# An attention and feed-forward kernel: from slot 8 on, the value products stand ahead of the scores

## The reference

```
sim = einsum('bhnid,bhnjd->bhnij', q * scale, kw)   # kw: token 0 and the 5 blocks around
attn = softmax(where(mask, -max, sim))
attn = einsum('gh,bhnij->bgnij', w_th, attn)        # the heads are mixed
out = einsum('bhnij,bhnjd->bhnid', attn, vw)
return out @ w_out + b_out
```

## Time and profile before

| | us |
|---|---|
| time, median of 3 runs | 244.66 (244.61 to 244.81) |
| profiled execution, its time | 244.73 |
| its span, from the first to the last instruction | 242.9 |
| PE busy | 225.3 |
| DVE busy | 177.2 |
| ACT busy | 162.9 |
| POOL busy | 93.2 |
| mean granted clock of TensorE, as a share of the full one | 0.988 |

### The profile page before, as it was taken

The page is one execution under the profiler, slowest core; times in us unless marked ns, Lnnn a source line. Parts: engine busy times, 40 slices in busy tenths (PEclk is TensorE's granted clock), DMA queues, the critical chain, the costliest instruction groups (busy, mean ns, idle before and its releaser), DMA issues.

```text
span 242.9 us, 10011 instructions
## 1 busy us (share of the span) xinstructions
PE 225.3 (93%) x4343; PEld 201.6 (83%) x4343; DVE 177.2 (73%) x461; ACT 162.9 (67%) x311; POOL 93.2 (38%) x111
## 2 busy tenths in 40 slices
PE   7899979999999999999999999998999988989970
PEld 6799869888999999888988888887988877889850
DVE  0774889987777882688667785678567899785874
ACT  2685557776656558975597559884697453888772
POOL 7035205532333351544425254534435264101452
PEclk9999999999999999999999999999999999999995
DMA  6937560020020001100200101010200101000003
GB/s 214 276 97 207 172 150 7 13 57 0 3 58 12 24 3 39 35 26 3 65 3 4 47 25 46 3 46 4 65 6 0 49 3 43 4 0 26 3 3 86
DMA packets 19107, 11.69 MB, mean 48 GB/s; under 512 B 2232, under 2 KB 18168, under 8 KB 18936
## 3 DMA queue, kind: packets, MB, share of 16 engines
q1 hardware_dynamic: 18324, 10.47, 15.3%
q10 hardware_dynamic: 740, 0.59, 0.8%
HBM read 8.91 MB, written 2.10 MB: 45 GB/s over the span
## 4 chain that ended last, share of the span: by engine, by line
PE 56%; DVE 18%; ACT 16%; issue 4%; DMA 2%; POOL 2%; POOLq 0%; SPq 0%; DVEq 0%; ACTq 0%
PE bank L1106 9%; PE bank L1108 8%; PE bank L1107 8%; PE bank L1255 7%; PE bank L1229 6%; DVE CTl L874 5%; PE bank L1213 3%; ACT CTh L577 3%; DVE AT L879 2%; ACT Yb L577 2%; DMA xq<-in_L_attn_x 2%; ACT L668 2%; DVE mx L886 2%; ACT gT L668 2%; PE bank L1299 2%
## 5 line engine op out<-in xcount | busy, mean ns | idle before, releaser
L874 DVE TENSOR_TENSOR CTl<-bank,CTh 128x512 fp32r<-128x512 f32 x64 | 41.0, 682 | 25.3 <-ACT CTh L577 25.1
L577 ACT ACTIVATE Yb<-bank 128x512 f32<-128x512 f32 x64 | 38.4, 600 | 28.3 <-PE bank L1108 27.7
L519 POOL TENSOR_TENSOR E<-E,rc 128x400 f32<-128x400 f32 x32 | 28.4, 889 | 75.5 <-DVE rc L896 75.3
L1106 PE MATMUL bank<-xTh,Gh 128*128 128x256 f32 x128 | 39.7, 310 | 1.7 <-ACT Yb L577 1.4
L720 ACT ACTIVATE E<-E 128x400 f32<-128x400 f32 x32 | 17.3, 539 | 32.1 <-DVE E L888 32.1
L1106 PE MATMUL bank<-CTh,Mh 128*128 128x256 f32 x128 | 37.0, 289 | 1.0 <-DVE CTl L874 1.0
L577 ACT ACTIVATE CTh<-bank 128x512 fp32r<-128x512 f32 x64 | 34.7, 600 | 2.4 <-PE bank L1255 2.4
L1108 PE MATMUL bank<-CTh,Ml 128*128 128x256 f32 x128 | 36.1, 282 | 0.0
L1107 PE MATMUL bank<-CTl,Mh 128*128 128x256 f32 x128 | 36.0, 281 | 0.0
L1107 PE MATMUL bank<-xTl,Gh 128*128 128x256 f32 x128 | 35.8, 279 | 0.0
L1108 PE MATMUL bank<-xTh,Gl 128*128 128x256 f32 x128 | 35.7, 279 | 0.0
(11 more groups left out here) (142 smaller groups left out, 465.0 us busy)
## 6 DMA issues: line engine op xcount, KB each, us to landing
raw<-in_L_attn_x SPq DMA_DIRECT2D x37, 64.0 KB
pt_rows<-PT SPq DMA_DIRECT2D x2, 512.0 KB, 5.3
R<-pt_rows SPq DMA_DIRECT2D x1, 1024.0 KB, 5.0
xr<-in_L_attn_x SPq DMA_DIRECT2D x6, 128.0 KB
out<-y SPq DMA_DIRECT2D x6, 128.0 KB, 1.9
raw<-in_L_attn_x SPq DMA_DIRECT2D x13, 56.0 KB
w_sb<-in_L_attn_w_qkv SPq DMA_DIRECT2D x2, 256.0 KB, 4.8
w_sb<-in_L_attn_w_qkv ACTq DMA_DIRECT2D x2, 256.0 KB, 4.6
```

What stands on the lines that cost most here:

```text
L519: tt(e, e, rc[s % 2][:, :].unsqueeze(2).broadcast_to([P, TILES, WIN]), ALU.mult).then_inc(s_norm, 1)
L577: copy = lambda o, i, **k: nc.scalar.activation(o, i, ACT.Copy, **k)
L874: v.tensor_tensor(ct_view(CTl[s // 4 % 2], s % 4, q), c_view(s, q), ct_view(f32(CTh[s // 4 % 2][:, :, :]), s % 4, q), ALU.subtract).then_i ...
L1106: mm(o, wh, rh, start=start, stop=False, **k)
```

## The change

`TURN = 7` is new. Up to slot 6 nothing changes; slot 7 does the old and the new beginning of work once each. From slot 8 on the order inside a slot is:

- TensorE: `c_part(s - 2)`, `scores(s)` with chunk n's square sum between the score products and the mask when k = 5, `transposes(s - 1)`, feed-forward pieces, `queries(s, 0)`, `o_part`, `down`, `queries(s, 1)`, `x1_T`.
- ScalarE: `ct_hi(s - 2)`, `at_hi(s - 1)`, `y_out(s, 0)`, `squares` when k = 4, Exp, `gelu` when k = 2, `y_out(s, 1)`, the rest.
- VectorE: `ct_lo(s - 2)`, `shift(s)`, `hidden_sum` when k = 5 (it now waits for `down_back` too, which writes the same bank), `at_lo(s - 1)`, `input_scale` and `up_input`, `second_sum` for n = 3, `total(s)`, the rest.

Transposes thus come one slot after their scores, no longer two. Behind the loop only `c_part(30)`, `transposes(31)` and `c_part(31)` are left, and `c_part(31)` takes the two spare banks that slot 30's took. What waits for what else is as it was, the wait for `s_O` in `ct_hi` among it.

```diff
+TURN = 7
         def c_bank(s, q):
-            return bank[(0, 2)[q] if s == 30 else C_BANK[q]]
+            return bank[(0, 2)[q] if s == 31 else C_BANK[q]]
 ...   ScalarE's loop
-                if s > LAG:
+                if LAG < s <= TURN:
                     ct_hi(s - LAG - 1)
-                if 0 < s < O_LAG:
+                if 0 < s < TURN:
                     y_out(s, 0)
-                if s >= LAG:
+                if LAG <= s <= TURN:
                     at_hi(s - LAG)
-                if s == 0 or s >= O_LAG:
+                if s == 0 or s == TURN:
                     y_out(s, 0)
-                if s < O_LAG:
+                if s >= TURN:
+                    ct_hi(s - 2)
+                    at_hi(s - 1)
+                if s > TURN:
+                    y_out(s, 0)
+                if s < TURN:
                     y_out(s, 1)
+                for n, k in ffn(s):
+                    if k == 4 and n < 4:
+                        squares(n, 0)
+                        squares(n, 1)
                 e = E[s % 2][:, :, 0:WIN]
                 act.wait_ge(s_sub, s + 1)
                 nc.scalar.activation(e, e, ACT.Exp).then_inc(s_exp, 1)
-                if s >= O_LAG:
+                for n, k in ffn(s):
+                    if k == 2 and n < 4:
+                        gelu(n, 0)
+                        gelu(n, 1)
+                if s >= TURN:
                     y_out(s, 1)
 ...
-            at_hi(30)
-            ct_hi(29)
+            ct_hi(30)
+            at_hi(31)
             gelu(4, 0)
-            at_hi(31)
-            ct_hi(30)
+            ct_hi(31)
             gelu(4, 1)
-            ct_hi(31)
 ...   VectorE's loop
-                if s > LAG:
+                if LAG < s <= TURN:
                     ct_lo(s - LAG - 1)
-                if s >= LAG:
+                if LAG <= s <= TURN:
                     at_lo(s - LAG)
+                if s > TURN:
+                    ct_lo(s - 2)
+                shift(s)
+                if s == TURN:
+                    ct_lo(s - 2)
                 for n, k in ffn(s):
-                    if k == 5 and n == 3:
+                    if k == 5:
+                        dve.wait_ge(f_back, n + 1)
                         hidden_sum(n)
+                if s >= TURN:
+                    at_lo(s - 1)
                 for n, k in ffn(s):
                     if k == 1:
                         input_scale(n)
                         up_input(n)
-                shift(s)
 ...   TensorE
-            def scores(s):
+            def scores(s, sums=()):
 ...
+                for n in sums:
+                    pe.wait_ge(f_dS, n + 1)
+                    square_sum(n)
 ...
-                need(pe, s_CTl, 60 if s == 31 else 2 * s if s < 30 else 0)
-                if s == 30:
+                need(pe, s_CTl, 2 * s if s < 31 else 0)
+                if s == 31:
 ...   TensorE's loop
-                if 0 < s < O_LAG:
+                if 0 < s < TURN:
                     queries(s, 0)
-                if s >= LAG:
+                if LAG <= s <= TURN:
                     transposes(s - LAG)
-                scores(s)
+                if s > TURN:
+                    c_part(s - 2)
+                scores(s, [n for n, k in ffn(s) if k == 5])
+                if s > TURN:
+                    transposes(s - 1)
 ...
-                if s == 0 or s >= O_LAG:
+                if s == 0 or s >= TURN:
                     queries(s, 0)
-                for n, k in ffn(s):
-                    if k == 5:
-                        square_sum(n)
-                if s == O_LAG:
+                if s == TURN:
+                    c_part(s - 2)
+                    transposes(s - 1)
 ...
                 for n, k in ffn(s):
                     if k == 4 and n < 4:
                         down(n)
+                queries(s, 1)
+                for n, k in ffn(s):
                     if k == 1:
                         x1_T(n)
-                queries(s, 1)
 ...
-                if s >= LAG:
+                if LAG <= s < TURN:
                     c_part(s - LAG)
 
-            transposes(30)
-            o_part(6, 1)
             c_part(30)
             transposes(31)
+            o_part(6, 1)
             o_part(6, 2)
             c_part(31)
```

More of the change, by code:

```diff
@@ L730, in _ @@
                         down_out(n)
-                        squares(n, 0)
-                        squares(n, 1)
                     if k == 1:
@@ L737, in _ @@
                         hidden_high(n, 1)
-                    if k == 2 and n < 4:
-                        gelu(n, 0)
-                        gelu(n, 1)
                     if k == 8 and n < 3:
                         result(n)
-            at_hi(30)
-            ct_hi(29)
+            ct_hi(30)
+            at_hi(31)
             gelu(4, 0)
-            at_hi(31)
-            ct_hi(30)
+            ct_hi(31)
             gelu(4, 1)
-            ct_hi(31)
             x1_hi(5)
@@ L1016, in _ @@
                         up_input(n)
-                shift(s)
                 for n, k in ffn(s):
-                    if k == 5 and n < 3:
-                        hidden_sum(n)
                     if k == 5 and n == 3:
@@ L1059, in _ @@
                         second_norm(n)
-            at_lo(30)
-            ct_lo(29)
+            ct_lo(30)
             at_lo(31)
-            ct_lo(30)
             ct_lo(31)
```

## The result

| | us | ratio to before |
|---|---|---|
| before, median of 4 runs | 244.63 (244.11 to 244.81) | |
| changed, median of 4 runs | 263.08 (259.35 to 265.33) | 1.066 (1.058 to 1.074) |
| changed, profiled execution | 262.44, span 260.6 | |

The change makes the kernel slower, by 6.6% in the ratio and by 18.4 us between the medians; 253.8 was forecast, in a range from 247.5 to 258.5. The direction was right and the size was not.

A forecast was written before the change was run, and what follows sets the result against it. TensorE, busy 93% of the span, was taken to set the pace, with evacuations close behind. Slots 8 to 27 +6.5, slot 7 +0.5 and the end +2.1 sum to +9.1, giving 253.8 us, range 247.5 to 258.5.

The forecast's parts named there:

- plain slot: A loop slot without feed-forward work on TensorE: 5.26 us instead of 5.41, 0.15 less, bounds 0 and 0.3.
- square sums: Slots 16, 20, 24 and 28, between scores and mask: 0.55 us instead of 0.84, 0.29 less each.
- turning in slot 7: Slot 7: the value products move ahead of the output part and wait for at_lo(5), charged +0.5 us.
- slots 8 to 27: Main loop: shorter slots -3.0, square sums -0.9, old waits -6.9, new waits +2.3, five waits +15.0; together +6.5 us.
- end up to T(31): Slots 28 up to transposes(31): the transposes wait for normalising of the slot just before; +0.9 us.
- from T(31) on: After transposes(31): output part (6,1), 1.42 us, now stands there, and the last value products lose 0.2 of waiting; +1.2.
- the five waits: Slots 10, 14, 18, 22 and 26: ct_hi waits for s_O; 8.26 us against 5.26, 3.0 lost each, 15.0 together.
- waits that go and new ones: Slots 8 to 27: old waiting and fringe removed, 6.9 us less; late softmax, up_input and ct_hi add 2.3.
- Clock: Rival, 4%: 2.2 us stands halve TensorE's clock, second query part and value products take twice as long; 8.5 more, 262.3.
- Recovery: Rival, 18%: each wait for s_O costs only 2.26 us, the next slot's slack absorbs VectorE's lateness; 248.0.
- Softmax a slot late: Rival, 12%: transposes wait for normalising in feed-forward slots too, a dozen slots by 0.35; 4.2 us more, 258.0.
- Faster: Rival, 8%: the wait for the output part costs little, so the change is worth -5.9 us; 238.8.

The follow-up runs named there:

- early output parts: Changed kernel with output parts one slot earlier and stage(n), n under 5, at the head of ScalarE's slot; 245.19 us, ratio 0.997.
- filled waits: Changed kernel with 18 useless products ahead of the second query part in slots 10, 14, 18, 22 and 26; 256.96 us, ratio 1.049.
- output parts placed better: Early output parts with moved tail, plus part 5 spread over slots 28 and 29, stage(n) after ct_hi, stage(6) earlier; 242.53 us, ratio 0.990.
- tail only: Changed kernel with one edit, output part (6,1) ahead of transposes(31); 260.91 us, ratio 1.064.
- half-filled kernel: Changed kernel with 9 useless products instead of 18 in each of the five waits; 260.19 us, ratio 1.059.
- kernel before with the waits: Kernel before, order unchanged, with the second query part waiting for normalise(s) in slots 10, 14, 18, 22 and 26; 271.52 us, ratio 1.107.

## Why the prediction was wrong

**The mechanism was right.** `ct_hi` of slots 10, 14, 18, 22 and 26 waits for the output part of the same slot and holds `y_out` and `at_lo` back. Foreseen were 2.26 and 0.66 of waiting (0.74 by its own lengths, since 6.70 and 0.82 are 7.52 and not 7.6) and 8.26 for such a slot; measured are 2.15 to 2.2, 0.57 and 8.26 to 8.32. The early output parts removed it.

**The plain slot** was put at 5.26 from 5.41; it is 5.20 (T takes 0.36 there, where 0.41 was put). The square sums between S and mask were put at 0.55; from 116.24, where S(16) starts in the changed kernel, to 117.64, where the mask product starts, it is 1.40, so 0.56.

**The terms outside the clock** against the trace, each as the difference from before: turning in slot 7 +0.5 foreseen, +0.97 measured; slots 8 to 27 +6.5 foreseen, +13.4 measured, of which 6.4 are slots 11, 23 and 27 at half clock (8.16 - 5.43, 7.93 - 6.68, 9.12 - 6.68); the end up to T(31) +0.9 foreseen, +0.6 measured; from T(31) on +1.2 foreseen (O(6,1) stands there), +2.7 measured, of which 1.5 are at half clock (4.96 - 3.46). Together 17.7, the difference of the spans. Take 6.4 and 1.5 away and 9.8 is left, where the sum had 9.1. Part of that is luck. In slots 8 to 27, 7.0 is left against 6.5: the shorter plain slot gives 1.2 more than the sum had (20 times 0.06), the five waits cost 0.4 more (8.26 to 8.32 against 5.20), and the other terms together, waits that go and new ones, came out 1.3 worse than put.

**The step that failed** is the pace of TensorE behind the waits. The sum charges each stand with its length and goes on at 0.12 a product. The rival *Clock* had the mechanism and named the places, but I gave it 4%, and the argument against it was poor. That its 262.3 comes so near is luck in part: it had Q1 and C slow at all five places for 8.5 us, while in the trace Q1 ran at full pace, C and what follows it (in slot 22 only what follows it) were slow at three of the five (6.4), and 1.5 more came at T(31). That a wait of 1.0 left the clock at full says nothing of 2.2 followed by 0.57. The earlier trace rows could not tell it either way, since no stand of that length was in the loop, so the unknown should have been bounded: 0 to 5 x 1.7 = 8.5 on top of the forecast, half of it in the middle. That gives 258 and a range that reaches 262. The Trainium skill, TensorE: Matmul & The Clock Gate, Why this matters for your kernels, says that a TensorE that is idle between bursts of products goes back to half clock. The trace agrees on the effect (the granted clock is 0.50 from 80 to 84 us, behind the stand of slot 10), but here shorter gaps than the one named there were enough: 2.2 and 0.57 us. The filled waits show that this, and no second wait, is the missing 7.9 us: with them slots 11, 23 and 27 and the end behind T(31) take what they take at full clock, though at T(31) no products were put in.

**The other rivals.** *Recovery* fell, since C waited for `AT` each time. *Softmax a slot late* fell in the loop: T waits for GpSimd only from slot 29 on, as the sum had it (0.2, 0.5, 1.0 and 1.7). *Faster* fell, and its price was not borne out either: 5.9 had been put for the new order without the wait. With the wait gone it was worth nothing that could be measured (0.997, 0.994 to 1.001), and 2.5 us with the output parts placed better.

**What stays open.** Why a stand of 2.15 us lowers the clock in some of the five places and not in others, and why that changes from one execution to the next, no run here shows. Nor is it shown why a stand of 1.67 us at T(31) lowered the clock in the changed kernel and not in the filled one.

## What to carry to other kernels

When work moves forward in one engine's queue, go through every semaphore that it waits for, the reuse of double buffers above all, and ask in which slot that semaphore is raised now. What is queued behind the waiting instruction pays, and whoever needs its bank. Where a plan puts a stand of one or two microseconds into a busy TensorE, price the products behind it at half pace for a few microseconds as an upper bound. A wait that can't be removed can be filled with products that nobody reads; here that gave back 4 to 6 us, and taking the wait away 17 to 18.

## What the runs showed of the hardware

- A TensorE that stood 2.2 us, worked 0.7 and stood 0.57 was at 1.2 GHz afterwards in three of five places (changed kernel), four of five (tail only), and two of five where the first stand was 1.1, in one profiled execution each. After a stand of 1.67 at T(31) it fell in the changed and the half-filled kernel and did not in the filled one. Behind the four stands of 4.25 of the kernel before with the waits, and behind its one of 2.3, it fell every time. In the changed kernel one fall in the loop cost 2.7, 1.3 and 2.4 us (slots 11, 23 and 27 against the filled kernel).
- Useless products in the stand kept the clock full in the loop, and the mean clock of the four runs was 0.973 to 0.983, against 0.932 to 0.955 without them; the gain was 6.1 us between the medians and 4 in the ratios. With half as many the mean clock was 0.966 to 0.973, and the time is not clearly different from none.
- From the last full-width product to the first 64-row one, and from the last 64-row product to the first 32-column one, 0.21 us pass instead of 0.12 (changed kernel, slot 10); from the last score product to the mask 0.14. Four transposes take 0.59 to the next 32-column product and 0.36 to 0.41 to the next full-width one.
